# Projection stage: the stores of a block's values are issued from ScalarE's queue instead of SyncE's

## The reference

```python
h = _layernorm(x) * (1 + ca) + sa
x = x + ga * attention(h)      # 16 heads of 16, causal, with latent down and up projections and rope on half a head
h = _layernorm(x) * (1 + cb) + sb
x = x + gb * experts(h)        # top 2 of 12, 8 real experts with a hidden width of 512, 4 pass x through
```

```python
q_lat = (x @ Wq_down).reshape(b, t, H, L);  q_c, q_e = q_lat @ Wq_up_c, q_lat @ Wq_up_e
k_lat = (x @ Wk_down).reshape(b, t, H, L);  k_c, k_e = k_lat @ Wk_up_c, k_lat @ Wk_up_e
v = einsum((x @ Wv_down).reshape(b, t, H, L), Wv_up)
q, k = concat(q_c, rope(q_e)), concat(k_c, rope(k_e))
```

## Time and profile before

| | us |
|---|---|
| three executions, median (lowest to highest) | 2499.7 (2498.16 to 2499.99) |
| the profiled execution's own time | 2493.01 |
| its span, first to last instruction | 2491.3 |
| projection with the first maxima, to the barrier | 0 to 283.9 |
| mean granted TensorE clock, share of full speed | 0.962 |

### The profile page before, as it was taken

One profiled execution on the slowest core, in us unless ns is written; L12 is line 12 of the kernel. 1 busy time (PEld: TensorE's weight loads), 2 busy tenths in 40 slices (PEclk: granted clock), 3 DMA queues, 4 the chain that ended last, 5 costly groups with the idle time before them and its releaser, 6 DMA issues. The chain is left out here.

```text
span 2491.3 us, 84848 instructions
## 1 busy us (share of the span) xinstructions
PE 2322.0 (93%) x34552; PEld 1577.5 (63%) x34553; DVE 1894.9 (76%) x3219; ACT 1659.7 (67%) x2983; POOL 766.4 (31%) x894
## 2 busy tenths in 40 slices
PE   6989589999999999999999999999989889999998
PEld 3555245556565655655655555655548879899897
DVE  5887778888888888888888888888828843555665
ACT  1666356787787787787877877877875455455554
POOL 2445301121111211211211111111114767676554
PEclk8999689999999999999999999999999899999999
DMA  5698563352443534534434433321238765665665
GB/s 178 195 245 239 146 107 92 75 124 78 97 103 80 104 92 96 103 85 92 101 89 101 98 85 82 80 59 42 59 88 252 239 156 120 106 133 112 100 102 87
DMA packets 224654, 287.95 MB, mean 116 GB/s; under 512 B 29462, under 2 KB 177974, under 8 KB 223926
## 3 DMA queue, kind: packets, MB, share of 16 engines
q1 hardware_dynamic: 185308, 235.53, 38.1%
q0 software_dynamic: 31872, 41.30, 9.8%
q10 hardware_dynamic: 7136, 6.32, 0.8%
HBM read 143.37 MB, written 138.81 MB: 113 GB/s over the span
## 5 line engine op out<-in xcount | busy, mean ns | idle before, releaser
L243 DVE TENSOR_REDUCE mxc<-ps 128x2 f32<-128x1024 f32 (+4 forms) x1168 | 1288.8, 1147 | 221.4 <-PE ps L230 142.9
L1201 ACT ACTIVATE probs<-ps 128x512 f32<-128x512 f32 (+1 forms) x2240 | 1170.8, 591 | 364.1 <-PE ps L1153 344.6
L1169 PE MATMUL ps<-probs,vs 128*32 128x512 f32 (+3 forms) x5120 | 611.4, 531 | 3.1 <-ACT probs L1201 1.8
L1153 PE MATMUL ps<-qs,ks 99*32 99x512 bf16 (+3 forms) x7040 | 564.8, 354 | 8.7 <-issue 4.3
L230 PE MATMUL ps<-ks,qs 96*32 96x512 bf16 (+11 forms) x7040 | 512.4, 351 | 49.4 <-DVE mxc L243 34.6
L1081 POOL TENSOR_SCALAR_AFFINE_SELECT probs<-probs 128x512 f32<-128x512 f32 x256 | 161.7, 634 | 723.0 <-ACT probs L1201 721.2
L1153 PEld LDWEIGHTS ps<-qs,ks 99*32 99x32 bf16 x7040 | 236.2, 97 | 219.6 <-issue 92.5
L230 PEld LDWEIGHTS ps<-ks,qs 96*32 96x32 bf16 x7040 | 224.9, 98 | 212.9 <-DVE mxc L243 82.1
L1153 PE MATMUL ps<-shared 99*32 99x512 bf16 (+3 forms) x3200 | 257.3, 351 | 0.2
L1930 PE MATMUL ps<-x_t,w_at 128*128 128x128 f32 x1968 | 242.1, 277 | 0.0
L1169 PEld LDWEIGHTS ps<-probs,vs 128*32 128x32 f32 x5120 | 197.8, 110 | 66.7 <-ACT o_sb L1193 10.4
(11 more groups left out here) (175 smaller groups left out, 2351.2 us busy)
## 6 DMA issues: line engine op xcount, KB each, us to landing
ks<-k_parts SPq DMA_DIRECT2D x66, 256.0 KB, 4.4
qs<-q_parts SPq DMA_DIRECT2D x66, 256.0 KB, 4.4
xs<-slot_x SPq DMA_DIRECT2D x126, 131.0 KB
v_ones<-vout SPq DMA_DIRECT2D x64, 256.0 KB, 3.9
vs<-v_ones SPq DMA_DIRECT2D x64, 256.0 KB, 3.5
attn_t<-o_sb SPq DMA_DIRECT2D x64, 256.0 KB, 2.6
slot_x<-zero SPq DMA_DIRECT2D x48, 262.0 KB, 2.7
q_parts<-parts SPq DMA_DIRECT2D x96, 128.0 KB, 2.5
```

What stands on the lines that cost most here:

```text
L243: return dve.tensor_reduce(mxc[:, h0:h0 + nh, i, c], unit_view(ps, u, at), AX_X, ALU.max)
L1153: ins = pe.matmul(o[at_q, h, :], ks[r][0:SROWS + MROWS, h0 + h, j * P + at_q.start:j * P + at_q.stop], qs[r][0:SROWS + MROWS, h0 + h, J * ...
L1169: ins = pe.matmul(o_ps[SLOT * g:SLOT * (g + 1), lo:QJ], vs[:, r, j, SLOT * g:SLOT * (g + 1)], probs[:, (NKT * r + m) % NPB, g, 0:QJ - lo], ...
L1201: act.activation(probs[:, (NKT * r + m) % NPB, h0:h0 + nh, 0:QJ - lo], st_view(r, s), ACT.Exp, scale=DH ** -0.5).then_inc(exp_done, 1)
```

## The change

`store` on SyncE loses its wait for `vcopy_done` and the four value stores of a block. A new step `store_values` on ScalarE does both, with lag 3, placed last in the turn: after `split` of the same block. Semaphores, buffers, sizes, destinations and the waits of L558 stay as they are. In all, 64 DMAs and 16 waits change their engine.

```diff
                 def store(b, j):
                     par, tok = j % 2, j * BLK
-                    sp.wait_ge(vcopy_done, BPS * b + j + 2)
-                    for n in range(TPB):
-                        dst = d["v_ones"][bass.ds(b, 1), :, :, TPB * j + n, :]
-                        sp.dma_start(dst.rearrange("o g p n -> (o p) g n"),
-                                     vout[:, par, n, :, :].rearrange("p (g h) s -> p g (h s)", g=NG)).then_inc(st_v[par], 16)
                     sp.wait_ge(low_done, 2 * (BPS * b + j) + 2 + 4)
...
+                def store_values(b, j):
+                    t, par = BPS * b + j, j % 2
+                    act.wait_ge(vcopy_done, t + 2)
+                    for n in range(TPB):
+                        dst = d["v_ones"][bass.ds(b, 1), :, :, TPB * j + n, :]
+                        act.dma_start(dst.rearrange("o g p n -> (o p) g n"),
+                                      vout[:, par, n, :, :].rearrange("p (g h) s -> p g (h s)", g=NG)).then_inc(st_v[par], 16)
+
...
-                staged(act, (0, norm), (1, modulate), (2, copies), (3, split), peeled=1)
+                staged(act, (0, norm), (1, modulate), (2, copies), (3, split), (3, store_values), peeled=1)
```

## The result

The changed kernel is slower: 2512.78 us (median of four executions, 2512.24 to 2517.27) against 2498.95 us for the kernel before (four, 2498.16 to 2499.99). The ratio is 1.0059 with an interval of 1.0042 to 1.0076. I had predicted 2510.5 us.

A forecast was written before the change was run, and what follows sets the result against it. Prediction: a loop through VectorE and ScalarE's root and L553 bounds turns 3 to 8; loads and transfers join in turns 9 to 14. Terms +9.6 +2.5 +1.4 +0.5 -3.2 = +10.8 on 2499.7 give 2510.5 us, range 2499 to 2521.

The forecast's parts named there:

- The sum for the projection: All terms from turn 3 to the projection's end, later stages taken as unchanged: +10.8 us.
- my costs of the turns: Time lost in the projection's turns: +9.6 us in 3 to 8, +2.5 in 9 to 11, +1.4 in 12 to 14.
- my signs: Signs of being right, among them turns 4 to 8 of 14.3 to 15 us and `xin` issues of 0.8 to 1.5 us.
- Turns 3 to 8: Turns set by a chain through VectorE: stores and `xin` issue delay ScalarE, 1.6 us a turn, +9.6 in all.
- The `xin` issue: ScalarE's load issue behind the four value stores: 1.0 us instead of 0.38, so 0.6 more a turn.
- The chain through the root: Turns 3 to 8: VectorE's last subtraction, root, L553 and rotation follow without slack; the root comes 0.9 us later.
- Turns 9 to 14: Turns with `ks` and `qs` loads: +2.5 us in turns 9 to 11 and +1.4 in turns 12 to 14.
- The rival of values that land early: Turns 9 to 14: on ScalarE's queue the 26.2 us of waits for values go; 2492.9 us in all; chance 0.07.
- The end: SyncE's last part stores, freed of 2.76 us of value stores and 0.4 of a held issue: -3.2 us.
- so all of it counts: Stage end: VectorE finishes 4.40 us ahead of the barrier, so the full 3.2 us saved on SyncE shortens the stage.
- the first rival: ScalarE's queue fills with the four stores and each `xin` issue waits for room: +21.9 us, 2521.6; chance 0.17.
- my last sign: Stages after the projection: a change of more than 2 us there would be something not seen.

The follow-up runs named there:

- e6: The changed kernel run again, against the kernel before: ratio 1.0034 (1.0014 to 1.0054).
- e2: Against the kernel before, two of a block's four value stores issued from ScalarE at the turn's end, two left on SyncE: ratio 0.9987 (0.9974 to 0.9999).
- e3: The kernel before with three useless 512-column copies on ScalarE at the end of each turn, no stores moved: ratio 1.0021 (1.0004 to 1.0038).
- e7: The changed kernel with the four value stores moved behind ScalarE's L544 (`h_t`) of the next turn; against the kernel before: ratio 1.0087 (1.0056 to 1.0119).
- e1: The changed kernel with ScalarE's value stores moved inside `split`, between the two pairs of casts; against the kernel before: ratio 0.9999 (0.9984 to 1.0014).
- e5: The kernel before, all stores on SyncE, each block's values issued ahead of the previous block's parts: ratio 0.9975 (0.9956 to 0.9994).
- e11: e1 with the `xin` loads moved from ScalarE's queue to SyncE's; against the kernel before: ratio 0.9961 (0.9949 to 0.9973).
- e9: e5 with the `xin` loads moved from ScalarE's queue to SyncE's; against the kernel before: ratio 1.0017 (1.0001 to 1.0034).

## Why the prediction was right, and where it was not

**The sign and the mechanism held.** ScalarE's list stands on the loop, the stores at the end of a turn hold it, and the relieved list of SyncE is worth nothing in the turns. The sum for the projection, +10.8, is near the measured +9.5 (e6: +9.9 to +11.0 against the two executions of the kernel before). The median's +13.8 carries the scatter of the later stages. That the sum came so near is in part luck: against the first table my costs of the turns were 4.5 us too high and the gain at the end 2.5 too high, and the two errors stand against each other. Of my signs, only two of turns 4 to 8 took 14.3 us or more (they took 13.86 to 14.59), and no `xin` issue in them took 0.8 us.

**Turns 3 to 8, 1.6 a turn predicted, 1.07 measured in the light turn and 1.18 on average.** The stores held the list for 2.33 us, not 2.65. The register instructions cost what I took, some 0.12 us a store beyond SyncE's gaps (0.16 us between two issues against 0.04), but the issues themselves were shorter, 1.86 us together against 2.19 on the idle SyncE queue. The root is 0.80 later (predicted 0.9). The `xin` issue is the mis-sized term: 0.62 us (0.24 more), where I took 1.0 (0.6 more). I had read it off issues on a loaded SyncE queue. e2, with two stores ahead, gives it alone, 0.22.

**The chain through the root was wrong.** I named two steps of ScalarE on the loop, the root and L553. Only the second proved to be: e3 moves the root by 0.71 and the turn by 0.25, e7 leaves the root and lengthens the turn by 1.8. My row had VectorE's normalising right behind the root, and I took its 2.98 us as fixed; it gave back all of the delay. The number didn't suffer, because the list hands the root's delay on to `h_t` undiminished when the stores stand ahead of both.

**Turns 9 to 14, +3.9 predicted, +1.9 measured from root to root, +4.3 in e6.** The rival of values that land early had its first step right: the waits for values went, from 26.2 to 2.4 us. What it promised did not come, because the held list took their place (roots at D + 3.24 to D + 3.85 against D + 1.83); e1 shows the gain when it doesn't (78.3 against 83.7). But it isn't the queue that brings it: e5 gets 77.9 on SyncE's.

**The end, -3.2 predicted, -0.6 measured** in the issues (18.17 us for the last 24 part stores against 18.69 us with four value stores among them), -0.2 from turn 15 to the barrier, -0.8 to -1.1 from POOL's last subtraction to the barrier. The step "so all of it counts" failed: I let the issues left in SyncE's list cost what they had cost, and they took longer once the values went out from ScalarE. 8.09 and 6.19 us for six stores, against 3.83, show it; why, stays open.

**The held issues** of the first rival came singly for `xin` (1.92 us in turn 9, 0.37 to 0.64 in the nine others of turns 3 to 12), not in every turn; but the stores themselves were held at the end of turns 8 to 11, 2.85 to 3.56 us, which is a part of what it said. And my last sign, a later stage that changes by more than 2 us, was too fine: the kernel before moves by 7 and 11 there.

**The start** is 0.8 us longer in the first table, but that is scatter: the root of turn 3 falls at 61.35 and 62.02 in the two executions of the kernel before, at 62.13 and 61.21 in those of the change.

**Open:** what holds the issues, where e1's 5 us and e11's rest went, and what makes the later stages scatter as they do.

## What to carry to other kernels

A DMA issue is free on an engine only where its list waits anyway. So look for the place in the list ahead of an idle time, behind work already started, not for the engine with the lowest busy share; the same stores on the same queue cost 1.07 us a light turn in one place and 0.03 in another. When a transfer is waited for, first try to issue it earlier, and only then on another queue. And where issues take longer than on an idle queue, taking some away need not shorten the list: here the others took longer instead.

## What the runs showed of the hardware

ScalarE's list runs ahead of its arithmetic, and an issue holds the first without the second: in e1 two stores are issued during L548 though L553 and L568 stand between it and them in the list. Back to back, four stores of 256 KB held the list for 2.33 us in the light turns, and six of 128 KB held SyncE's for 3.8. In the turns with the loads of `ks` and `qs` two stores took 5.24 us in e11 and six took 8.88 in e9, most of it in one issue (4.09 and 5.64). A VectorE instruction beside POOL's subtraction took 2.01 us instead of 0.40, and the group ended at D + 5.36 for roots from D + 1.83 to D + 3.4. The expense of an instruction in a timeline can therefore shrink without any gain.
